# Graph convolution summed from high and low halves, first column half for all nodes, then the second; counts turned and degrees made in the relation stage

## The reference, cut to what matters

```python
mean = agg.reshape(34, n, -1) / jnp.maximum(cnt, 1.0).reshape(34, n, 1)
h1 = jnp.einsum('nri,rio->no', mean, W_rel) + h @ W_root + b_rgcn
xw = h1 @ W_gcn
deg = segment_sum(ones, dst) + 1.0
dinv = rsqrt(deg); norm = dinv[src] * dinv[dst]
out = segment_sum(xw[src] * norm[:, None], dst) + xw * (dinv * dinv)[:, None]
x = x + out + b_gcn
```

## Time and profile before

| | before |
|---|---|
| median of 3 runs | 2304.84 us (2297.58 to 2315.82) |
| profiled execution: its time / its span | 2306.32 us / 2304.6 us |
| mean granted TensorE clock | 0.939 of full |
| TensorE matmul busy | 1985.8 us, 86% |
| VectorE busy | 1225.5 us, 53% |
| ScalarE busy | 835.6 us, 36% |
| GpSimd busy | 553.7 us, 24% |

### The profile page before, as it was taken

One profiled execution on the slowest core, in us unless ns is written; L12 is line 12 of the kernel. 1 busy time (PEld: TensorE's weight loads), 2 busy tenths in 40 slices (PEclk: granted clock), 3 DMA queues, 4 the chain that ended last, 5 costly groups with the idle time before them and its releaser, 6 DMA issues.

```text
span 2304.6 us, 34640 instructions
## 1 busy us (share of the span) xinstructions
PE 1985.8 (86%) x11182; PEld 1720.6 (75%) x11183; DVE 1225.5 (53%) x2242; ACT 835.6 (36%) x1117; POOL 553.7 (24%) x538
## 2 busy tenths in 40 slices
PE   3999898979999989689999999967788687778885
PEld 2988896759999967589999999954475665648663
DVE  5761224454434645755555555545543876655873
ACT  1222222322222223235555555533330276213763
POOL 0002765530000066343343331017600000000000
PEclk9999999999999999899999999979988799785998
DMA  3555567745555487558888878758810111001111
GB/s 109 163 158 164 164 165 256 264 140 156 167 164 183 158 287 242 168 171 276 270 265 272 274 267 283 253 172 290 266 40 0 37 52 66 5 28 36 52 46 39
DMA packets 203272, 378.40 MB, mean 164 GB/s; under 512 B 18810, under 2 KB 173626, under 8 KB 203176
## 3 DMA queue, kind: packets, MB, share of 16 engines
q1 hardware_dynamic: 170520, 246.23, 33.2%
q0 software_dynamic: 31216, 128.89, 17.7%
q10 hardware_dynamic: 1440, 1.97, 0.2%
HBM read 288.68 MB, written 88.34 MB: 164 GB/s over the span
## 4 chain that ended last, share of the span: by engine, by line
PE 36%; DVE 7%; DMA 5%; issue 5%; ACT 3%; ACTq 0%; POOL 0%; another core or an unknown queue 0%; SPq 0%; DVEq 0%; POOLq 0%
PE ps L1728 18%; PE ps L1942 4%; DMA arena<-in_L_gnn_W_rel 3%; PE ps L1907 2%; PE ps L1628 2%; PE ps L1757 2%; PE ps L1870 1%; PE ps L1978 1%; ACT arena L792 1%; DMA arena<-U,ix 1%; PE ps L1993 1%; PE ps L1623 1%; PE ps L1548 1%; DVE arena L1361 1%; DVE al L1365 1%
## 5 line engine op out<-in xcount | busy, mean ns | idle before, releaser
L1728 PE MATMUL ps<-w_hi,hT_hi 128*128 128x384 f32 x2052 | 722.0, 352 | 38.5 <-ACT arena L585 14.6
L1728 PE MATMUL ps<-w_hi,hT_lo 128*128 128x384 f32 x2052 | 696.6, 339 | 0.0
L1728 PE MATMUL ps<-w_lo,hT_hi 128*128 128x384 f32 x2052 | 696.0, 339 | 0.0
L1728 PEld LDWEIGHTS ps<-w_hi,hT_hi 128*128 128x128 f32 x2052 | 393.5, 192 | 48.8 <-issue 17.8
L1728 PEld LDWEIGHTS ps<-w_lo,hT_hi 128*128 128x128 f32 x2052 | 393.8, 192 | 0.1
L1728 PEld LDWEIGHTS ps<-w_hi,hT_lo 128*128 128x128 f32 x2052 | 392.4, 191 | 0.0
L499 POOL DMA_INDIRECT arena<-U,ix x252 | 269.2, 1068 | 469.3 <-DMA U<-arena 350.5
L585 ACT ACTIVATE arena<-ps 128x384 f32<-128x384 f32 x160 | 78.2, 492 | 454.4 <-PE ps L1728 391.6
L1628 PE MATMUL ps<-arena,onehot 128*128 128x512 f32 x504 | 195.1, 511 | 18.1 <-DMA arena<-U,ix 10.1
L909 DVE TENSOR_TENSOR w_lo<-arena,w_hi 128x2304 fp32r<-128x2304 f32 x45 | 114.9, 2555 | 112.6 <-ACT w_hi L578 111.2
L1628 PEld LDWEIGHTS ps<-arena,onehot 128*128 128x128 f32 x504 | 89.9, 196 | 95.5 <-issue 91.6
(11 more groups left out here) (260 smaller groups left out, 3033.9 us busy)
## 6 DMA issues: line engine op xcount, KB each, us to landing
arena<-in_L_gnn_W_rel SPq DMA_DIRECT2D x74, 1152.0 KB, 6.3
U<-arena SPq DMA_DIRECT2D x292, 192.0 KB
arena<-in_L_gnn_W SPq DMA_DIRECT2D x36, 1152.0 KB
U<-z SPq DMA_DIRECT2D x28, 864.0 KB
arena<-rows_d SPq DMA_DIRECT2D x42, 320.0 KB, 3.4
arena<-in_L_gnn_root SPq DMA_DIRECT2D x4, 1152.0 KB
arena<-U,ix POOLq DMA_INDIRECT x252
arena<-in_L_gnn_W_root SPq DMA_DIRECT2D x2, 1152.0 KB
```

Source lines behind the costliest of these rows:

```text
L1728: ins = pe.matmul(acc, l, r[:, j, kt, :], start=(n == 0), stop=(n == 3 * KT - 1))
```

## The change

- The sums of the graph convolution are made in fp32r from high and low halves of both sides: `cg_hi`, `cg_lo` of the turned counts, `rg_hi`, `rg_lo` of dinv * xw. ScalarE scales while it evicts, VectorE makes the low half from the same bank, and only then is the bank free (`evac` now counts there).
- The identity product goes: `own_edge` adds the identity to the diagonal blocks of CT and subtracts it again afterwards.
- The order of the ten sums is the first column half for all five groups, then the second, in four banks (`GA`) instead of two.
- C is turned in the last pair of the relation stage, five transposes after each of the first five products, and `deg` and its square root are made at the end of `further`, before the messages.
- The first sums' part of the eviction lets `transpose(3)` begin (`acc_out` 5, then 6 from the third block on). The bias of x is added by groups; C is masked in the middle of the sums; the first split for `Q_G1` comes after the ten products.

```diff
+GA = 4
...
+        with nc.sbuf_tensor("rg_hi", [P, NG, D], F32R) as rg_hi:
+            pass
         h = sb("h", [P, NG, D])
+        with nc.sbuf_tensor("rg_lo", [P, NG, 780], F32R) as rg_lo:
+            pass
         R = sb("R", [P, NG, 780])
...
+        with nc.sbuf_tensor("arena_r", [P, 6528 + GB * D], F32R) as arena_r:
+            pass
         arena = sb("arena", [P, 6528 + GB * D])
+        cg_hi, cg_lo = (arena_r[:, 4608 + NG * NP * i:4608 + NG * NP * (i + 1)].rearrange("p (g n) -> p g n", g=NG) for i in range(2))
...
                                 act.wait_ge(S["steps"], S_REL + 4 * TC * it + k + 11)
                                 act.wait_ge(u_st[TC * j + g], 16 * (2 * it + rr + st))
                                 act.activation(ust[:, TC * j + g, :], ps[:, g, 0:HALF], cp).then_inc(S["evac"], 1)
+                                if last and k < NG:
+                                    act.wait_ge(S["ct_tp"], k + 1)
+                                    act.activation(CT[:, k, :], psf[:, 2048:2048 + NP], cp).then_inc(S["ct_cp"], 1)
                                 if TC * j + g < 3 and not end:
                                     hc_part(it + rr, 1 - rr, TC * j + g)
...
                 split(0, Q_GCN)
+                act.wait_ge(S["deg_ok"], 1)
+                act.activation(std[:], deg[:], ACT.Sqrt).then_inc(S["deg_sq"], 1)
...
             messages(2)
 
-            for s in range(NG):
-                act.wait_ge(S["ct_tp"], s + 1)
-                b = 4 + 2 * (s % 2)
-                act.activation(CT[:, s, :], psf[:, 512 * b:512 * b + NP], cp).then_inc(S["ct_cp"], 1)
-            act.wait_ge(S["deg_ok"], 1)
-            act.activation(std[:], deg[:], ACT.Sqrt).then_inc(S["deg_sq"], 1)
             transpose(3, cp)
+
+            def counts_hi(s):
+
+                act.wait_ge(S["deg_ok"], 2)
+                act.activation(cg_hi[:, s, :], CT[:, s, :], cp).then_inc(S["ct_cp"], 1)
+
+            def gcn_hi(k, g):
+
+                act.wait_ge(S["steps"], 5 * (Q_GCN + k) + g + 11)
+                act.activation(rg_hi[:, g, k * HALF:(k + 1) * HALF], ps[:, (Q_GCN + k + g) % 2, 0:HALF], cp,
+                               scale=dinv[:, g:g + 1]).then_inc(S["gcn_y"], 1)
+
+            split(0, Q_GCN + 1)
+            for k in range(2):
+                for g in range(NG):
+                    if k == 0:
+                        counts_hi(g)
+                    gcn_hi(k, g)
+            split(0, Q_G1)
...
-            dense(Q_GCN, lambda g, k: R[:, g, k * HALF:(k + 1) * HALF])
...
                 split(0, Q_GCN)
+                link(dve.tensor_reduce(deg[:], C, AX.X, ALU.add))
+                link(dve.tensor_scalar(deg[:], deg[:], 1.0, None, ALU.add))
+                dve.sem_inc(S["deg_ok"], 1)
...
                     else:
                         ins = dve.tensor_tensor(h[:, :, c0:c1], R[:, :, c0:c1], sums(c0), ALU.add)
+                        if c0 == 0:
+                            ins.then_inc(S["acc_out"], 1)
                 ins.then_inc(S["acc_out"], 1)
...
             further()
             messages(2)
-            sums_out(2)
-            dve.wait_ge(S["acc_out"], 5)
-
-            link(dve.tensor_reduce(deg[:], C, AX.X, ALU.add))
-            link(dve.tensor_scalar(deg[:], deg[:], 1.0, None, ALU.add))
-            dve.sem_inc(S["deg_ok"], 1)
-            dve.wait_ge(S["ct_tp"], NG)
-            dve.tensor_scalar(C, C, 0.0, NEG, ALU.is_equal, ALU.mult)
             dve.wait_ge(S["deg_sq"], 1)
             link(dve.reciprocal(dinv[:], std[:]))
+            sums_out(2)
+            dve.wait_ge(S["acc_out"], 6)
             transpose(3, False)
+            split(0, Q_GCN + 1)
+
+            def own_edge(op):
+
+                for g in range(NG):
+                    d = CT[:, g, P * g:P * (g + 1)]
+                    ins = dve.tensor_tensor(d, d, ident[:], op)
+                link(ins)
+            own_edge(ALU.add)
+            dve.sem_inc(S["deg_ok"], 1)
+            dve.wait_ge(v_in[1], 32)
             for k in range(2):
-                if Q_GCN + k + 1 < Q_SPLIT[Q_GCN]:
-                    split(0, Q_GCN + k + 1)
-            dve.wait_ge(v_in[1], 32)
-            dve.tensor_tensor(x[:], x[:], vec[:, 1, :].unsqueeze(1).to_broadcast([P, NG, D]), ALU.add).then_inc(S["vec_ok"], 1)
+                for g in range(NG):
+                    cols = slice(k * HALF, (k + 1) * HALF)
+                    dve.wait_ge(S["gcn_y"], NG * k + g + 1)
+                    dve.scalar_tensor_tensor(rg_lo[:, g, cols], ps[:, (Q_GCN + k + g) % 2, 0:HALF], dinv[:, g:g + 1],
+                                             rg_hi[:, g, cols].bitcast(F32), ALU.mult, ALU.subtract).then_inc(S["evac"], 1)
+                    if k == 0:
+                        dve.wait_ge(S["ct_cp"], NG + g + 1)
+                        dve.tensor_tensor(cg_lo[:, g, :], CT[:, g, :], cg_hi[:, g, :].bitcast(F32), ALU.subtract).then_inc(S["ct_lo"], 1)
+                    else:
+                        ins = dve.tensor_tensor(x[:, g, :], x[:, g, :], vec[:, 1, :], ALU.add)
+            ins.then_inc(S["vec_ok"], 1)
             dve.wait_ge(S["vec_ok"], 4)
-            dve.wait_ge(S["evac"], 5 * (Q_GCN + 2) + 2)
-            for g in range(NG):
-                dve.tensor_scalar(R[:, g, 0:D], R[:, g, 0:D], dinv[:, g:g + 1], None, ALU.mult).then_inc(S["gcn_y"], 1)
+            own_edge(ALU.subtract)
+            split(0, Q_G1)
             for i in range(2 * NG):
-                j, cols = i // 2, slice((i % 2) * HALF, (i % 2 + 1) * HALF)
-                if j and i % 2 == 0:
+                c, j = i // NG, i % NG
+                cols = slice(c * HALF, (c + 1) * HALF)
+                if c and j:
                     dve.wait_ge(S["gcn_ev"], i)
                     stats(j - 1)
                 dve.wait_ge(S["gcn_mm"], i + 1)
-                ins = dve.scalar_tensor_tensor(x[:, j, cols], ps[:, 2 + i % 2, 0:HALF], dinv[:, j:j + 1], x[:, j, cols], ALU.mult, ALU.add)
-                ins.then_inc(S["gcn_ev"], 1)
+                dve.scalar_tensor_tensor(x[:, j, cols], ps[:, 2 + i % GA, 0:HALF], dinv[:, j:j + 1], x[:, j, cols],
+                                         ALU.mult, ALU.add).then_inc(S["gcn_ev"], 1)
+                if i == NG - 1:
+                    dve.tensor_scalar(C, C, 0.0, NEG, ALU.is_equal, ALU.mult)
             dve.wait_ge(S["gcn_ev"], 2 * NG)
...
             def transpose(k, half_done=None):
                 for kt in range(KT):
                     b = 2 * (kt % 2)
+                    if k == 3 and kt == 2:
+                        pe.wait_ge(S["acc_out"], 6)
...
+                def counts_turned(s):
+
+                    if s == 0:
+                        pe.wait_ge(S["acc_out"], 4)
+                    else:
+                        pe.wait_ge(S["ct_cp"], s)
+                    for g in range(NG):
+                        ins = pe.transpose(psf[:, 2048 + P * g:2048 + P * (g + 1)], C[:, g, P * s:P * (s + 1)], ident[:])
+                    ins.then_inc(S["ct_tp"], 1)
...
                                 product(ps[:, g, 0:HALF], hc[rr], j, slice(P * g, P * (g + 1))).then_inc(S["steps"], 1)
                                 if TC * j + g < 3 and not (last and rr == 1):
                                     hc_part(it + rr, 1 - rr, TC * j + g)
+                                if last and k < NG:
+                                    counts_turned(k)
...
             def further():
+                pe.wait_ge(S["ct_cp"], NG)
...
             transpose(3)
             pe.wait_ge(S["hT_lo"], 4 * KT)
             for k in range(2):
                 for g in range(NG):
                     step(0, Q_GCN + k, g)
-            pe.wait_ge(S["gcn_y"], NG)
-            pe.wait_ge(S["ct_cp"], NG)
             for i in range(2 * NG):
-                j, cols = i // 2, slice((i % 2) * HALF, (i % 2 + 1) * HALF)
-                if i >= 2:
-                    pe.wait_ge(S["gcn_ev"], i - 1)
-                acc = ps[:, 2 + i % 2, 0:HALF]
+                c, j = i // NG, i % NG
+                if j == 0:
+                    pe.wait_ge(S["evac"], 5 * (Q_GCN + c + 1) + 2)
+                if i >= GA:
+                    pe.wait_ge(S["gcn_ev"], i - GA + 1)
+                n = 0
                 for s in range(NG):
-                    pe.matmul(acc, CT[:, s, P * j:P * (j + 1)], R[:, s, cols], start=(s == 0), stop=False)
-                pe.matmul(acc, ident[:], R[:, j, cols], start=False, stop=True).then_inc(S["gcn_mm"], 1)
+                    if i == 0:
+                        pe.wait_ge(S["ct_lo"], s + 1)
+                    for l, r in ((cg_hi, rg_hi), (cg_hi, rg_lo), (cg_lo, rg_hi)):
+                        ins = pe.matmul(ps[:, 2 + i % GA, 0:HALF], l[:, s, P * j:P * (j + 1)], r[:, s, c * HALF:(c + 1) * HALF],
+                                        start=(n == 0), stop=(n == 3 * NG - 1))
+                        n += 1
+                ins.then_inc(S["gcn_mm"], 1)
```

(4 more changed lines are left out.)

## The result

The changed kernel takes 2291.2 us (median of 20 runs, 2281.8 to 2300.0), the kernel before 2306.3 (20 runs, 2297.6 to 2318.1): ratio 0.9925, interval 0.9909 to 0.9942. Of 2306.3 us that ratio is 17.3 us less (13 to 21); the two medians lie 15.0 apart. The forecast was 20.0 less. Runs of one kernel lie 18 to 20 us apart, so small terms can't be read from whole times; they are read here from the distances between marks of the profiles. The profiled execution of the changed kernel has a span of 2297.2 us, only 7.4 under that of before, because it reached the last pair of relations some 9.5 us later, in a part whose code the change leaves as it was.

What follows compares the result with a forecast made beforehand. TensorE and what it waits for were taken to bound the rewritten stretch. Terms -14.8 - 3.4 - 5.6 + 0.6 + 2.7 + 0.5 = -20.0 took 2306.3 to 2286.3 us, range 2274 to 2297.

Steps and rivals of the forecast that it cites:

- Part 1: Sums of the graph convolution: 120 fp32 records become 150 fp32r matmuls at 0.1725 us each, -14.8 us.
- D: Sums: weight loads not covered, 150 matmuls at whole record length 0.335 us, 24.4 us more, 2310.7 us; chance 0.05.
- E: Sums: fp32r runs at the rate of fp32 records, 0.322 us each, ending at 2308.7 us; chance 0.02.
- Part 2: Gap before the sums: TensorE's 3.41 us wait goes as scaling moves into the eviction, -3.4 us.
- Part 3: Between messages and products: turning of h starts earlier, -5.6 us; longer low clock in products costs +0.6 (0 to 1.25).
- Part 4: GCN products: same 180 matmuls, banks freed by ScalarE then VectorE in time, 0 us, at worst 1 us.
- rival B: Products and messages: TensorE waits for low halves (5 us), late degrees cost fully (+3.2), ending at 2294.5 us; chance 0.17.
- Part 5: Last pair of the relation stage: 25 count transposes on busy TensorE, +2.7 us, bounds 0 and 6.2.
- rival C: Relation stage and messages absorb additions (-3.2), turning of h partly at full clock (up to -3), 2280 to 2283; chance 0.16.
- Part 6: Degrees before messages: first one-hot 3.7 us late, mostly absorbed by the gathers' pace, +0.5 us, bounds 0 and 3.7.

Runs made afterwards that it cites:

- e5: Changed kernel's sums, but counts turned and degrees made after the messages, as in the kernel before; ratio 0.9925 to the kernel before.
- e8: Changed kernel with the sums in plain fp32 (100 records), no high and low halves of counts and rows; ratio 0.9942 to the kernel before.
- e6: Changed kernel with the sums in the old order, both column halves of a group, then the next group; ratio 0.9925 to the kernel before.
- e7: Changed kernel with two banks for the sums instead of four; ratio 0.9930 to the kernel before.
- e11: Changed kernel measured a third time, without edit; ratio 0.9931 to the kernel before.
- e10: Changed kernel with the degrees' reduce and addition in the relation stage, right after the counts are complete, measured again; ratio 0.9915 to the kernel before.
- e1: Changed kernel measured again, without edit; ratio 0.9897 to the kernel before.

## Why the prediction was right, part by part

| part | forecast | measured, changed against before |
|---|---|---|
| 1, sums (to the last group's statistics) | -14.8 | 26.95 - 41.35 = -14.4 |
| 2, gap | -3.4 | -3.4 |
| 3, eviction to first product | -5.6 | 13.02 - 18.41 = -5.4 |
| 3 and 4, products | +0.6 | 34.08 - 33.02 = +1.1 |
| 5, transposes in the last pair | +2.7 | 5 x 0.55 = +2.7 |
| 6, degrees before the messages | +0.5 | +3.0 (133.4 - 130.4; e5's set: 0.5 to 1.1) |
| sum | -20.0 | -16.4 |

The sum of the measured terms lies within the interval of the whole time (13 to 21 less). Each term is from one profile before and one after, and the last one is unsure by some 2 us, so that the agreement to a microsecond is in part luck.

**Part 1** held in its mechanism and nearly in size: 0.175 us against the assumed 0.1725, which is 0.4 us over 150. Rivals D and E fell: the sums' matmuls start 0.175 us apart, not 0.306. That each of the 150 has its own weight load did not lengthen this step. The step of the trace gave 25.9 us and the sums took 26.3. The estimate from the formula of the Trainium skill ("TensorE: Matmul & The Clock Gate", Back-to-back issue gap), 24.4 us, was further off. The 14.4 us have three sources: 6.0 from fp32r in place of fp32 (e8), 6.4 from the 20 identity records (20 x 0.322), and 2.0 because the sums no longer begin at a granted clock of 0.71 (40.7 against 38.7 at full clock). The prediction had them in one sum and named the clock without a price; e8 tests the first alone, and the other two are worked out from rows.

**Part 2** held, and e6 shows that the credit is not the order's. By elimination, what closed the gap is that scaling happens in the eviction: it is what the changed kernel, e6 and e8 have in common, and none of them has a gap. No run changed the scaling alone. e7's one stall, 1.20 us where 1.3 was expected, confirms the reckoning for VectorE's lateness.

**Part 3** held. The price at the start of the products was twice what I took (+1.1, inside the bounds 0 to 1.25). In e5, where the count transposes keep TensorE busy before them, the products take 32.9 us, as in the kernel before (33.0). But they took 32.9 in e8 too, with nothing there, so that the price isn't fixed.

**Part 4**: no idle time between groups, so no part of rival B's stall.

**Part 5** held to the rounding. It overlapped with nothing, and the turning of h (granted 0.50) gained no clock, so rival C got neither of its terms in the first profile.

**Part 6 is the term that was mis-sized**: I let 3.7 us of VectorE shrink to 0.5, because the gathers set the pace and had not yet waited for TensorE. In two sets of runs the early degrees made messages 3.8 and 3.9 us shorter, close to the upper bound, and the first two profiles differ by 3.0: that is rival B's piece. In the third set, e5 with no degrees before the messages was only 0.5 to 1.1 us shorter. So the term is larger than 0.5 in most comparisons, but its size is open between 0.5 and 3.9 us; each figure is a difference of two single profiles, and three kernels with the degrees in front (e6 to e8) differ by 0.6 among themselves. My argument looked only at the first dozen gathers. In the first profiles the 31st gather was already 2.3 us later, counted from the first (47.2 against 44.9), and the last 2.9 (124.4 against 121.5); but in e11 only 0.7 us were lost by the 51st (71.2 against 70.5 in e10) and 3.7 us by the last. By which wait a late first message travels down the stage is not shown.

One more thing the prediction did not see. It treated parts 3, 5 and 6 as separate bargains. Together the moves of counts and degrees gave back 3.7 us after the messages and cost 2.7 and 0.5 to 1.1 (e5), or about 3 by the first two profiles: they earn nothing that can be measured. The whole gain of the change comes from the sums and the gap, 17.8 us.

## What to carry to other kernels

Count what a matmul costs by the pace of its records, not by the number of products: three fp32r products with high and low halves (3 x 0.175 us) were cheaper than one fp32 product of two records (2 x 0.322 us), and a diagonal term can go into the operand. Before moving work forward to "idle" engines, look for what is queued behind it there: the same 3.5 us reduce stood in the way before the messages and in the relation stage as well. When an instruction delays the first item of a long pipelined stage, give its whole length a real chance as the price; the stage's average pace is no proof of slack.

## What the runs showed of the hardware that was not expected

The time at the lower clock at the start of the products differed between executions: the 180 products took 32.9 to 34.3 us with the same work ahead of them. In e8 (32.9) the granted clock was 0.50 in their first 3.0 us and 0.97 in the 3.8 after that, in e1 (34.3) 0.50 and 0.59, and in both 1.00 afterwards. A 384-column copy with a scale for each partition took ScalarE 0.58 us where the plain one took 0.49; an addition of 128 columns took VectorE 0.29 us against 0.22 for the copy.
